# Routing tables by scatter beside the output projection, and the projection's inputs loaded during the attention

## The reference

```python
h = x + _attention(_rmsnorm(x, ln1_w), wq, wk, wv, wo)      # the last factor is  @ wo.T
h = h + _moe(_rmsnorm(h, ln2_w), gate_w, w1, w2, w3)

def _moe(x, gate_w, w1, w2, w3):                            # 8 experts, inner width 512
    logits = xf @ gate_w.T
    rw, sel = jax.lax.top_k(logits, 2)
    rw = softmax(rw)
    for e in range(8):
        we = sum(where(sel == e, rw, 0.0), axis=-1)
        h = silu(xf @ w1[e].T) * (xf @ w3[e].T)
        out = out + h @ w2[e].T * we[:, None]
```

## Time and profile before

| | |
|---|---|
| median of 3 runs | 3277.74 us (3275.07 to 3281.41) |
| the profiled execution | 3278.61 us |
| its span, first to last instruction | 3276.9 us |
| mean granted TensorE clock | 0.927 of full speed |
| busy: PE / DVE / ACT / POOL | 88% / 71% / 58% / 19% |

### The profile page before, as it was taken

How to read it: one execution, slowest core, us unless ns; L and a number is a source line. 1 busy time by engine, 2 the same in 40 slices (tenths; PEclk the granted TensorE clock), 3 DMA queues, 4 the chain that set the end, 5 groups by cost and what they waited for, 6 DMA issues and landing times. The chain is left out here.

```text
span 3276.9 us, 64323 instructions
## 1 busy us (share of the span) xinstructions
PE 2891.2 (88%) x22812; PEld 1808.9 (55%) x22813; DVE 2334.1 (71%) x3783; ACT 1884.4 (58%) x3407; POOL 616.5 (19%) x983
## 2 busy tenths in 40 slices
PE   5888888884999999999999999969569999999970
PEld 4666677663333333333333333347458888888860
DVE  5676666763999999999999999646774444444436
ACT  3555565550688888888888888813233333333320
POOL 1122212121000000000000000011233444444430
PEclk8889988996899999999999999978789999999985
DMA  1323323323122222222222222168321111111129
GB/s 36 116 85 100 115 102 115 114 81 113 56 67 67 67 67 67 72 70 69 70 72 68 67 67 67 45 208 302 97 89 42 51 50 50 51 50 50 50 76 371
DMA packets 191429, 292.58 MB, mean 89 GB/s; under 512 B 31976, under 2 KB 118272, under 8 KB 191248
## 3 DMA queue, kind: packets, MB, share of 16 engines
q1 hardware_dynamic: 147184, 212.38, 20.7%
q0 software_dynamic: 18176, 52.45, 4.8%
q10 hardware_dynamic: 25888, 25.30, 2.3%
HBM read 159.94 MB, written 127.93 MB: 88 GB/s over the span
## 5 line engine op out<-in xcount | busy, mean ns | idle before, releaser
L819 DVE TENSOR_REDUCE b_mxq<-b_p_m 128x1 f32<-128x1024 f32 x1024 | 1222.3, 1223 | 72.1 <-PE b_p_m L841 65.1
L758 ACT ACTIVATE b_probs<-b_p_e 128x512 f32<-128x512 f32 x2048 | 1105.5, 597 | 148.4 <-PE b_p_e L889 39.8
L841 PE MATMUL b_p_m<-b_kst,b_qst 64*128 64x512 f32 x2048 | 765.5, 454 | 27.9 <-DMA b_vst<-v_d 23.7
L889 PE MATMUL b_p_e<-b_qst,b_kst 64*128 64x512 f32 x2048 | 747.8, 444 | 0.2 <-ACT b_probs L758 0.2
L860 PE MATMUL b_p_o<-b_probs,b_vst 128*32 128x256 f32 x8208 | 642.6, 390 | 0.5 <-ACT b_probs L758 0.4
L889 PEld LDWEIGHTS b_p_e<-b_qst,b_kst 64*128 64x128 f32 x2048 | 315.9, 184 | 419.7 <-ACT b_probs L758 355.3
L1489 ACT ACTIVATE d_act<-d_p_up 128x512 f32<-128x512 f32 x136 | 81.3, 597 | 486.8 <-PE d_p_up L1551 486.8
L841 PEld LDWEIGHTS b_p_m<-b_kst,b_qst 64*128 64x128 f32 x2048 | 320.0, 188 | 59.0 <-DVE b_mxq L819 30.9
L860 PEld LDWEIGHTS b_p_o<-b_probs,b_vst 128*32 128x32 f32 x8208 | 168.3, 108 | 324.4 <-issue 187.0
L1566 PE MATMUL d_p_y<-w2T,d_hT 128*128 x1096 | 258.7, 379 | 0.8 <-ACT d_hT L1483 0.8
L1504 DVE TENSOR_SCALAR d_xh<-d_p_x,d_ln 128x128 fp32r<-128x128 f32 x272 | 82.9, 346 | 238.0 <-PE d_p_x L1545 238.0
(11 more groups left out here) (267 smaller groups left out, 4026.1 us busy)
## 6 DMA issues: line engine op xcount, KB each, us to landing
b_qst<-qk_d SPq DMA_DIRECT2D x384, 64.0 KB
b_kst<-qk_d SPq DMA_DIRECT2D x384, 64.0 KB
x1y_d<-a_x1y SPq DMA_DIRECT2D x32, 512.0 KB, 4.2
qk_d<-a_hi SPq DMA_DIRECT2D x32, 512.0 KB, 2.8
qk_d<-a_lo SPq DMA_DIRECT2D x32, 512.0 KB, 3.7
v_d<-a_v_s SPq DMA_DIRECT2D x16, 1024.0 KB, 6.9
b_vst<-v_d SPq DMA_DIRECT2D x64, 256.0 KB
o_d<-b_oT POOLq DMA_DIRECT2D x64, 256.0 KB
```

The costliest lines, as they stand in the source:

```text
L758: nc.scalar.activation(probs[(2 * step + e % 4 // 2) % BUFS][:, (e % 2) * 512:(e % 2 + 1) * 512], p_e[(slot(e) if more1 else e) % EB][:], ...
L819: V_.reduce_max(mxq[half][:, h, qt:qt + 1], p_m[j % 2][:], AX.X).then_inc(s["m_red"], 1)
L841: mm(p_m[j % 2][:, kh * 512:(kh + 1) * 512], qst[r][rows(h), qt * P:(qt + 1) * P], kst[r][rows(h), kh * 512:(kh + 1) * 512], start=True, s ...
L889: mm(p_e[u % EB][:], kst[r][rows(h), kt * P:(kt + 1) * P], qst[r][rows(h), a * 512:(a + 1) * 512], start=True, stop=True).then_inc(s["e_ps ...
```

## The change

**In stage 2** the tiles that stage 3 reads first live through both stages (`ProjectionTiles`). SP, no longer POOL, issues the 64 stores of `oT`, each behind the loads of its pair. Behind the last pair's part SP loads the weights, `xy` of half 0 and `oin` of both halves of batch 0, then does what it did before (sums, inverses), then loads the inverses `rd`, stores the last `oT` and waits for all of it. POOL and DVE build `ident` and `heads` at the stage's start.

**In stage 3** the loads and constants of the start are gone. A table `table_d` of 8 x 8192 entries in DRAM, one region for each expert, is filled with zeros. DVE gets two new steps in each half: `count` (one-hot of the choices, running counts) and `place` (the slot of each of the 8 x 128 choices of a half); PE gets two matmuls (`places`). POOL then writes the 128 code numbers of a column to their places in the table, one indirect DMA for each of 8 columns of a half, 4 bytes a partition: six behind the root of each half from half 3 on (78), and 50 behind the last half's. SP waits for all of them at the stage's end.

**Stage 4** becomes `tile_tables_and_weights`. The slots, the one-hot tiles and `p_inv` are gone. DVE works out from the counts, in some 25 small steps, which row of the table belongs to each tile, POOL fetches the rows with two indirect DMAs, and PE turns them. For the weights PE has six PSUM banks; ACT makes the rounded copy and half of `w2T`, DVE subtracts directly from PSUM and makes the other half; POOL no longer takes part.

Stages 1, 5 and 6 are as before.

```diff
@@ softmax_attention, SP
+        def store(n):
+            sp.wait_ge(s["oT_done"], n + 1)
+            sp.dma_start(o_rows[n - 1], oT[n % 2][:]).then_inc(s[f"o_out{n % 2}"], 16)
...
                 load(pair + 3, (r + 3) % RING)
+            if pair > 0:
+                store(pair)
             if more1:
                 maxima((r + 1) % 2, (r + 1) % RING, pair * SLOTS + (NEG_AT + 4))
...
         pairs(sp, body)
-        sp.wait_ge(s["o_stored"], 16 * (PAIRS - 8))
+        load_weights()          # wo_raw, gw_raw, ln2, xy[0]: four DMAs
+        for k in range(2):
+            sp.wait_ge(s[f"o_out{k}"], 16 * (PAIRS - 8) // 2)
+        for half in range(2):
+            for k in range(2):
+                sp.dma_start(ahead.oin[half][:, k], ahead.o_rows(o_d)[0, half, 8 * k:8 * k + 8, 0:16, :]).then_inc(s["ahead_o"], 16)
         for n in range(BEFORE):
             sp.dma_start(den[:, n], ...).then_inc(s["den_in"], 16)
         sp.wait_ge(s["den_done"], 1)
         for k in range(2):
             sp.dma_start(rd_d[k, 0:n_batches - 1]..., den_part[k][:].bitcast(f32)).then_inc(s["den_out"], 16)
         sp.wait_ge(s["den_out"], 32)
+        for half in range(2):
+            for k in range(2):
+                sp.dma_start(ahead.rd[half][16 * k:16 * k + 16, :].bitcast(f32), rd_d[k, 0, half]).then_inc(s["ahead_o"], 16)
+        store(PAIRS)
+        sp.wait_ge(s["ahead_w"], 64)
+        sp.wait_ge(s["ahead_o"], 128)
+        for k in range(2):
+            sp.wait_ge(s[f"o_out{k}"], 16 * PAIRS // 2)
@@ softmax_attention, POOL
-            pool.wait_ge(s["oT_done"], pair + 2)
-            g.dma_start(o_rows[pair], oT[(r + 1) % 2][:]).then_inc(s["o_stored"], 16)
@@ output_projection_and_gate, SP (its start; the same for POOL's constants)
-        load_output(0, 0)
-        load_inverses(0, 0)
-        sp.dma_start(xy[0][:], x1y_v[0]).then_inc(s["in0"], 16)
-        sp.dma_start(wo_raw[:], ...)
-        sp.dma_start(gw_raw[:], gate_w).then_inc(s["w_in"], 16)
-            sp.dma_start(ln2[:], ...).then_inc(s["w_in"], 16)
-        load_output(1, 0)
-        load_inverses(1, 0)
...
+        sp.wait_ge(s["scat"], 16 * C * N)
@@ output_projection_and_gate, POOL
+        def scatter(at):
+            if at % C == 0:
+                pool.wait_ge(s["slot_i_done"], at // C + 1)
+            g.indirect_dma_start(table_d, bass.IndirectOffsetOnAxis(ap=slot_i[:, at:at + 1], axis=0), code[:, at:at + 1], None).then_inc(s["scat"], 16)
+        BESIDE = 6
         def body(n, half, b, b_next, before, after):
             pool.wait_ge(s["ms_done"], n * T + (T + 1))
             g.tensor_scalar(r_s[:], ms[:], EPS, None, ALU.add).then_inc(s["ms_eps"], 1)
             g.tensor_tensor(r_s[:], r_s[:], mhalf[:], ALU.pow).then_inc(s["r_done"], 1)
+            if n > 2:
+                for k in range(BESIDE):
+                    scatter((n - 3) * BESIDE + k)
         halves(pool, body)
+        for at in range((N - 3) * BESIDE, N * C):
+            scatter(at)
@@ output_projection_and_gate, DVE
+        def count(n):
+            V_.tensor_tensor(hot[r][:, :, 1:], chosen..., expert..., ALU.is_equal)        # 128x64
+            V_.tensor_tensor_scan(cum[r]..., within..., hot[r]..., 0.0, ALU.mult, ALU.add) # 128x72
+            V_.tensor_copy(hot[1 - r][:, :, 0], cum[r][:, :, C])                           # 128x8
+        def place(n):
+            V_.tensor_tensor(where[:], p5[:], hot[r][:, :, 1:], ALU.mult)                  # 128x64
+            V_.reduce_sum(slot[:], where[:].rearrange("p e c -> p c e"), AX.X)
+            V_.tensor_copy(slot_i[:, n * C:(n + 1) * C], slot[:]).then_inc(s["slot_i_done"], 1)
...
             if before:
                 choose(n - 1)
+            if n > 1:
+                place(n - 2)
+            if before:
+                count(n - 1)
             dve.wait_ge(s["r_done"], n1)
@@ output_projection_and_gate, PE
+            mm(p5[:], ones[:], cum[r][:, :, 0:C], start=True, stop=False)
+            mm(p5[:], lower[:], hot[r][:, :, 1:], start=False, stop=True).then_inc(s["slot_ps"], 1)
@@ tile_tables_and_weights (was route_and_transpose_weights)
 SP      for each expert: three loads of 512 KB, raw[j] behind the transposes of the expert before
+ACT     nc.scalar.copy(up_hi[...], p_w[j][:])   x4;   w2T[:, e, 0:2] <- p_w[4]
+DVE     V_.tensor_tensor(up_lo[...], p_w[j][:], up_hi[...].bitcast(f32), ALU.subtract)   x4;   w2T[:, e, 2:4] <- p_w[5]
+DVE     ahead of these, once: some 25 steps on 128x8 to 128x16, then cmp and ex on 128x1088
+POOL    indirect_dma_start x2 from table_d
+PE      24 transposes for each expert into p_w[0..5], each bank behind free{b} of the expert before
-DVE/PE  slots (lines 1305 to 1335), 128 columns (lines 1341, 1342, 1376), lines 1353 to 1362
-ACT     up_lo copy (line 1268);  POOL subtraction (line 1287)
```

More of the change, by code:

```diff
@@ L952, in output_projection_and_gate @@
     NT = 2 * n_batches * T
+    N = 2 * n_batches
+    REGION = NT * P
+    C = 2 * T
+    i32 = mybir.dt.int32
+    ones, lower = sb("ones", [P, P]), sb("lower", [P, P])
+    zeros = sb("zeros", [P, NE * REGION // P])
+    expert_i, expert = sb("expert_i", [P, NE], i32), sb("expert", [P, NE])
+    code_i, code = sb("code_i", [P, 2 * NT], i32), sb("code", [P, 2 * NT])
+    within = sb("within", [P, NE, C + 1])
+    chosen = sb("chosen", [P, T, 2])
+    hot, cum = [sb(f"hot{r}", [P, NE, C + 1]) for r in range(2)], [sb(f"cum{r}", [P, NE, C + 1]) for r in range(2)]
+    where, slot, slot_i = sb("where", [P, NE, C]), sb("slot", [P, C]), sb("slot_i", [P, N * C], i32)
     best = sb("best", [P, NT, 2])
@@ new lines, in tile_tables_and_weights @@
+    total, full, full_i, tiles, end = sb("total", [P, NE]), sb("full", [P, NE]), sb("full_i", [P, NE], i32), sb("tiles", [P, NE]), sb("end", [P, NE])
+    limit, skip, rise = sb("limit", [P, NE]), sb("skip", [P, NE]), sb("rise", [P, NE])
+    past, part = sb("past", [P, G, NE]), sb("part", [P, G, NE])
+    row, row_i, left = sb("row", [P, G]), sb("row_i", [P, G], i32), sb("left", [P, G])
+    cmp, ex = sb("cmp", [P, TILES, NE]), sb("ex", [P, TILES])
+    codes = [sb(f"codes{g}", [P, P]) for g in range(G)]
@@ L1282, in _ @@
[L1282 to L1287 removed]
+        g_ = nc.gpsimd
+        g_.memset(ident[:], 0.0).then_inc(s["id0"], 1)
@@ new lines, in _ @@
+        V_.tensor_tensor(rise[:, 0:NE - 1], limit[:, 1:NE], limit[:, 0:NE - 1], ALU.subtract)
+        then(V_.tensor_tensor(past[:], mine[:].rearrange("p (g o) -> p g o", o=1).to_broadcast([P, G, NE]), end[:].rearrange("p (o e) -> p o e", o=1).to_broadcast([P, G, NE]), ALU.is_ge))
+        last = NE - 1
+        then(V_.tensor_tensor(part[:, :, 0:last], past[:, :, 0:last], skip[:].rearrange("p (o e) -> p o e", o=1)[:, :, 0:last].to_broadcast([P, G, last]), ALU.mult))
+        then(V_.reduce_sum(row[:], part[:, :, 0:last], AX.X))
@@ new lines, in _ @@
+        then(V_.tensor_tensor(row[:], row[:], mine[:], ALU.add))
+        then(V_.tensor_scalar(row[:], row[:], float(ROWS - 1), None, ALU.min))
+        V_.tensor_copy(row_i[:], row[:]).then_inc(s["row_done"], 1)
+        then(V_.tensor_tensor(part[:, :, 0:last], past[:, :, 0:last], rise[:].rearrange("p (o e) -> p o e", o=1)[:, :, 0:last].to_broadcast([P, G, last]), ALU.mult))
+        then(V_.reduce_sum(left[:], part[:, :, 0:last], AX.X))
+        then(V_.tensor_scalar(left[:], left[:], limit[:, 0:1], None, ALU.add))
@@ L1368, in _ @@
-        pe.wait_ge(s["E_done"], 1)
-        for k in range(2):
-            rhs = E[:, k * NT:(k + 1) * NT, :].rearrange("p c e -> p (c e)")
-            mm(p_before[:, k, 0:W], before[:], rhs, start=True, stop=True)
-            i = mm(p_total[:, k, 0:W], ones[:], rhs, start=True, stop=True)
-        i.then_inc(s["ps"], 1)
-        def column(c, r, start, stop):
-            pe.wait_ge(s["hot"], c + 1)
-            mm(p_inv[:], is_lo[r][:], is_hi[r][:], start=start, stop=stop, skip_group_check=True).then_inc(s["inv_ps"], 1)
+        tr = nc.tensor.transpose
```

416 lines of the change are left out of this document (235 added, 181 removed).

## The result

The changed kernel takes 3388.23 us (median of four runs, 3381.05 to 3393.65) against 3278.47 for the kernel before (four runs). The ratio is 1.0334, with a 95% interval of 1.0311 to 1.0356: 110 us slower, where 24 us faster was predicted and the range ended at 3300. The profiled execution took 3381.05 us with a span of 3379.3.

A forecast was written before the change was run, and what follows sets the result against it. Stage 3 was taken as bound by nearly level PE and DVE chains, stage 4 by its 128 column steps. From 3278.61, -6.1 + 12.6 + 49.2 - 80.1 = -24.4 gave 3254.2 us, range 3234 to 3300.

The forecast's parts named there:

- the 78 transfers beside: nothing: Stage 3's halves: POOL's six transfers and root take 7.3 of 9.65 us, DMA queues 8.8, so no time is added.
- The list of what would prove it wrong: Signs against the forecast: transfers not spaced by POOL's busy time, 4-byte writes draining slowly, stage 4 waiting for non-loads.
- The new work in the halves, +12.6: Stage 3: six small DVE operations and two PE matmuls add 0.9 us to each of 14 halves.
- Behind the last half, +49.2: End of stage 3: 56 transfers at 0.99 us, POOL's drain of 5.1 and 1.2 make 62.1 us against 12.9.
- the serial rival: POOL's queue in stage 3: nothing hidden, each transfer costs 1.85 us, the whole 3340 us; chance 0.16.
- Stage 4, -80.1: Stage 4: column steps go, weight loads at 5.2 to 6.0 us an expert set the length; 51.5 us from 131.65.
- Begin of stage 3, -6.1: First projection of stage 3 comes 6.1 us earlier: 12.7 less at its start, 6.6 more at stage 2's end.
- The 12.7 of the hole: Start of stage 3: PE's first transpose starts with the stage, not 12.74 us later behind the last weight load.
- the 6.6 of the sum: End of stage 2: SP's sum loads queue behind the last store and the early loads, 6.6 us later.
- The ports: Stage 3: DVE's `base` and `xg` hold POOL up through the shared SBUF port, 3268 us in all; chance 0.10.
- Inputs not hidden: End of stage 2: SP's late sum loads could eat all 12.7 us of the hole; 3259 if `rd` lands 5 later.

The follow-up runs named there:

- e2: Changed kernel with the 78 transfers beside the halves turned into reads and all 128 writes behind the last half: 3394.6 us.
- e6: Changed kernel with its 4-byte writes 32 bytes apart (8 words a slot): 3271.8 us.
- e1: Changed kernel with all 128 transfers behind the last half, none beside: 3377.95 us.
- after: The changed kernel itself, against the kernel before: 3388.23 us, ratio 1.0334.
- e7: Kernel before with only stage 3's weights and inputs loaded ahead and the attention's stores on SP; stage 4 as before: 3276.97 us, ratio 0.9987.
- e11: Changed kernel, writes 32 bytes apart, sum loads ahead of weights, transfers one half earlier, six beside each half: 3269.21 us, 0.9972 of the kernel before.
- e12: Changed kernel, 256 KB table permuted so following slots lie 32 bytes apart over 32 KB and stretches are rewritten late: 3281.3 us.
- e3: Changed kernel with its 4-byte writes 64 bytes apart (16 words a slot): 3287.4 us.
- e5: Changed kernel, small table permuted so eight following slots lie in eight stretches of 64 bytes of one 512-byte row: 3327.6 us.
- e8: Changed kernel with its 4-byte writes 16 bytes apart (4 words a slot): 3277.1 us.
- e9: Changed kernel, small table permuted so sixteen following slots lie in sixteen stretches of 32 bytes: 3336.9 us.

## Why the prediction was wrong

**The step that failed: "the 78 transfers beside: nothing".** POOL's side came out (six transfers and a root fit into 9.65 us; e2 and e6 show halves of 9.61 and 9.65 with them), though with less slack than reckoned: at 1.26 a transfer six and the root take 8.9 and not 7.3. The DMA side was priced by packets of 256 bytes, 17.9 ns each. Here about sixteen writes of each transfer go to neighbouring words of one expert's list, and the next transfer goes on where they ended. Such writes hold up the DMA engines for everyone: 98 us over the 15 steps, by e1 (139.8 of 237.5) and again by e6 (140.5). The list of what would prove it wrong came near ("if 4-byte writes are slower to drain than POOL makes them (above 125 ns a packet, eight to a queue)"), but it looked for the cost in the writes' own packets, which took 21 ns, and no rival gave it a price, so the range could not hold it.

**The new work in the halves, +12.6.** Right: +9.8 in e1, +10.5 in e6.

**Behind the last half, +49.2: 31.9 too little, mostly in three terms.** From the first of the last 56 starts to stage 4 I had 61.9 (62.1 with the 0.2 ahead of it); it took 90.8. A transfer takes 1.26 and not 0.99 (56 x 0.27 = 15.1). It lies between my two bounds, 0.99 and the 1.85 of the serial rival, and I took the lower. POOL stands still once, 9.4 beyond a step (2.7 with sparse writes). And from the last start to stage 4 pass 11.8 against 7.3; with the writes 32 bytes apart (e6) it is 4.1, so dense writes still on their way are the likely reason. Another 3.2 lie ahead of the transfers: from the last product to the end of POOL's last root pass 18.4 us and not 15.2. With sparse writes the 90.8 would be 55 x 1.26 + 2.7 + 4.1 = 76; e6 has 76.4.

**Stage 4, -80.1.** Right: -75.8, and -76.2 in e6. Its columns were the bound, and the loads replaced them; in 2505 to 2545 of after this is PE's largest wait (sum, number, longest):

```profile
PE r_p_w L1510 <- DMA r_raw<-in_L_ffn_w_dram: 15.2, 15, 4.1
```

**Begin of stage 3, -6.1.** Right in kind: -2.9 in after, -5.1 in e7, -5.2 in e6. The 12.7 of the hole went; the end of stage 2 came later than the 6.6 of the sum, by 9.9 in after and 7.7 in e7, counted from the last copy. The late sum loads ate part of the hole; issued ahead of the weights they gave 3.7 back (e11).

**The other rivals.** The ports: right for `base`, which does hold transfers up, but at 0.3 us a half in e6 and hidden there; `xg` holds them hardly (1.02 us at the mean, not 0.96), and DVE waited for the root only once in e6's 2160 to 2300 (2.5 us). Inputs not hidden: PE's first transpose starts at 2141.92, with the stage. With the addresses cured and nothing else, e6 is at 3271.8 (one run), 18 above my 3254. So the sum was too low without the failed step as well: by 16.6 behind the last half (the spacing and the pause), 3.9 in stage 4 and 0.9 at its begin, less 2.1 in the halves.

## What to carry to other kernels

A scatter is priced by where its elements land as well as by their number: lists that are filled in order by elements of 4 bytes write the same few bytes again and again within microseconds. Give every element its own 32 bytes, or interleave the list so that its neighbours lie 32 bytes apart over a long stretch and the writing comes back late (e12: after about 90 us). When a queue of tiny packets shows a share of 1%, look at how long the packets of the other queues have become before you call it free. Where POOL issues transfers beside DVE, look at those that start under a DVE operation with both inputs in SBUF. Take the spacing of back-to-back instructions from two of the same kind in a row, or keep both bounds in the sum where no such row exists.

## What the runs showed of the hardware

- Writes of 4 bytes to DRAM that come back to the same place in the same transfer or the next ones slow the core's other DMA traffic: packets of loads 168 ns instead of 91 at the mean, of stores 107 instead of 48, with the engines shown busy and 79 GB/s moved. The same writes 32 bytes apart: 100 and 49 ns; 16 bytes apart, two to a stretch of 32: 0.85 us a half. The Trainium skill ("DMA: Bandwidth & Descriptors", section "Specifications") says that below 512 bytes the DMA engines do a read-modify-write; that alone doesn't tell these cases apart, since all of them write less than 512.
- Reads of 4 bytes at the same indices leave the halves at 9.61, as without any transfer beside them (e2).
- Indirect transfers of 128 elements follow each other on POOL every 1.26 us; the 0.30 between them was the same in every run.
- A transfer on POOL that starts while DVE adds two tiles of SBUF (`base`, 1.22 us) ends 0.83 us behind that addition, up to 1.93 us in place of 0.96 (e6).
- Behind the halves POOL stood still once in every kernel with these transfers, always ahead of the 114th of the 128 writes: 4.0 us from start to start with sparse writes (e3, e6, e12), 5.5 to 6.1 in e5, e8 and e9, 10.6 to 12.6 with the dense ones (after, e1, e2), also where 78 reads had gone ahead (e2). What it waits for was not found.
